# A decoder layer on one core: the first attention's steps dealt anew to the gaps between its groups' scores

## What is computed

```python
q = (x @ Wq).reshape(b, t, KV, G, D)
k = (x @ Wk).reshape(b, t, KV, D)
v = (x @ Wv).reshape(b, t, KV, D)
scores = jnp.einsum('bqhgd,bkhd->bhgqk', q, k) * scale
scores = jnp.where(causal_mask, scores, -jnp.inf)
w = jax.nn.softmax(scores, axis=-1)
y = jnp.einsum('bhgqk,bkhd->bqhgd', w, v)
x = _layernorm(x + y.reshape(b, t, H * D) @ Wo)
```

## Time and profile before

| | us |
|---|---|
| median of three runs | 1901.7 |
| the profiled execution | 1899.83 |
| its span | 1897.9 |
| TensorE busy | 1763.2 (93%) |
| VectorE busy | 1238.2 (65%) |
| ScalarE busy | 710.4 (37%) |
| GpSimd busy | 266.2 (14%) |

### The profile page before, as it was taken

How to read it: one execution, slowest core, us unless ns; L and a number is a source line. 1 busy time by engine, 2 the same in 40 slices (tenths; PEclk the granted TensorE clock), 3 DMA queues, 4 the chain that set the end, 5 groups by cost and what they waited for, 6 DMA issues and landing times.

```text
span 1897.9 us, 37020 instructions
## 1 busy us (share of the span) xinstructions
PE 1763.2 (93%) x14528; PEld 1448.6 (76%) x14528; DVE 1238.2 (65%) x1943; ACT 710.4 (37%) x1492; POOL 266.2 (14%) x237
## 2 busy tenths in 40 slices
PE   4888877799996999999999999999999999999997
PEld 3777765688885777878888888888888888888886
DVE  3667764668775556676676675665756766756776
ACT  4454542212121435353343343433433433434331
POOL 1444542534332000000000000000000000000000
PEclk8889988899998899999999999999999999999999
DMA  4111220100000203012020030020120200300011
GB/s 153 52 38 47 61 66 17 63 13 11 22 0 1 95 1 84 22 54 57 14 80 21 7 93 7 14 85 8 42 56 13 78 21 7 93 7 13 7 50 45
DMA packets 51082, 76.65 MB, mean 40 GB/s; under 512 B 9152, under 2 KB 27712, under 8 KB 50240
## 3 DMA queue, kind: packets, MB, share of 16 engines
q1 hardware_dynamic: 51008, 75.62, 13.3%
HBM read 68.78 MB, written 6.82 MB: 40 GB/s over the span
## 4 chain that ended last, share of the span: by engine, by line
PE 63%; DVE 2%; issue 2%; ACT 1%; POOLq 0%; POOL 0%; DVEq 0%
PE pair L1849 9%; PE pair L1850 9%; PE pair L1851 9%; PE y_ps L1849 3%; PE y_ps L1851 3%; PE y_ps L1850 3%; PE qa_ps L1849 3%; PE qa_ps L1851 3%; PE qa_ps L1850 3%; PE pair L1986 2%; PE pair L1977 2%; PE pair L1976 1%; PE pair L1985 1%; PE qd_ps L2053 1%; PE qd_ps L2054 1%
## 5 line engine op out<-in xcount | busy, mean ns | idle before, releaser
L1849 PE MATMUL pair<-XH,GUH 128*128 128x512 f32 x800 | 313.4, 392 | 0.0
L1850 PE MATMUL pair<-XL,GUH 128*128 128x512 f32 x800 | 312.3, 390 | 0.0
L1851 PE MATMUL pair<-XH,GUL 128*128 128x512 f32 x800 | 312.3, 390 | 0.0
L1849 PEld LDWEIGHTS pair<-XH,GUH 128*128 128x128 f32 x800 | 150.5, 188 | 32.3
L1851 PEld LDWEIGHTS pair<-XH,GUL 128*128 128x128 f32 x800 | 150.4, 188 | 32.2
L1850 PEld LDWEIGHTS pair<-XL,GUH 128*128 128x128 f32 x800 | 150.5, 188 | 31.6
L1413 POOL TENSOR_TENSOR qb_raw<-qb_raw,qb_scale 128x704 f32<-128x704 f32 x8 | 13.6, 1704 | 1057.7 <-DVE G L1567 923.4
L372 ACT ACTIVATE p<-scores_ps,nm 128x128 f32<-128x128 f32 (+1 forms) x256 | 104.1, 433 | 103.2 <-DVE nm L457 103.2
L1763 DVE TENSOR_TENSOR h<-pair,sg 128x512 f32<-128x512 f32 x80 | 55.2, 690 | 131.9 <-ACT sg L1512 130.2
L1423 ACT ACTIVATE HH<-h 128x512 fp32r<-128x512 f32 (+1 forms) x120 | 75.9, 633 | 170.5 <-DVE h L1768 94.0
L1567 DVE TENSOR_TENSOR HL<-h,HH 128x512 fp32r<-128x512 f32 (+1 forms) x120 | 83.4, 695 | 83.9 <-ACT HH L1423 83.9
(11 more groups left out here) (337 smaller groups left out, 4186.5 us busy)
## 6 DMA issues: line engine op xcount, KB each, us to landing
gu_raw<-in_gu SPq DMA_DIRECT2D x20, 512.0 KB, 3.8
wrep<-soft_f SPq DMA_DIRECT2D x64, 128.0 KB
dw_raw<-in_dw SPq DMA_DIRECT2D x10, 512.0 KB, 4.6
xT_raw<-in_xT SPq DMA_DIRECT2D x8, 512.0 KB, 4.1
x_raw<-in_x SPq DMA_DIRECT2D x8, 512.0 KB, 3.7
VR<-v_rows SPq DMA_DIRECT2D x32, 128.0 KB, 2.6
out<-xtok SPq DMA_DIRECT2D x4, 1024.0 KB, 4.3
gu_raw<-in_gu SPq DMA_DIRECT2D x10, 384.0 KB, 3.1
```

The lines of the kernel that those rows point to most:

```text
L1849: mm(out, wh, xh, start=first, stop=False)
L1850: mm(out, wh, xl, start=False, stop=False)
L1851: return mm(out, wl, xh, start=False, stop=last)
```

## The change

- **TensorE.** `vals(b)` and `queries(b, 1)` move into the batch itself, behind `scores(b, 0)`, followed by the transposes of batch b - 2. `values(b - 1)` moves behind `scores(b, 1)`. `queries(b + 1, 0)` and the first half of the output product stand behind `scores(b, 2)`, `keys(b + 1)` and the second half behind `scores(b, 3)`. `outputs` becomes `output(b, i)`, one half a call. Before the first scores stand `queries(0, 0)` and `keys(0)` alone.
- **VectorE.** The last group's work is finished in the next batch: `reciprocals(b - 1, 3, 1)` first of all, then `maxima(b, 0)`, the second residual of batch b - 2, and the probability turns of group 3. `probs_turned(b, 0, 0)` stands ahead of `reciprocals(b, 1, 1)`, `o_low` on both sides of `maxima(b, 2)`. The splits of the two weights for the next stage move from batch 0 to batch 1.
- **Semaphores.** `half_done` counts the first part of `values`, so that `probs_turned(b, 0, 0)` waits for that part and `probs_turned(b, 0, 1)` for the whole. `o_low` waits for its own `o_high`. `values` also waits for `values_copy`, the first queries of a batch for the first `o_low`, `context(1)` for the last `residual` of batch 6.
- **Banks.** Queries go to bank 0, keys and values to bank 1, output rows and their transposes to banks 2 and 3. `values` writes each bank's 256 columns in the order group, half, position, and `OH` and `OL` hold (group, half) blocks, so `o_high` and `o_low` each take two banks whole and no longer half of all four.
- **Queues.** ScalarE, GpSimd and SyncE follow the same order; `row_out` and `deviation` of the second half come a batch later. Batch 2 is unrolled too (the loop has 4 turns).

The core of the diff (a line "..." stands where lines are left out, removed ones among them):

```diff
@@ -150,7 +150,7 @@
 
         self.scores = ctx.enter_context(nc.psum_tensor("scores_ps", [P, 4, 512], F32))
         self.rest = ctx.enter_context(nc.psum_tensor("rest_ps", [P, 4, 512], F32))
-        self.projections = [self.rest[:, n, :] for n in (2, 3, 1)]
+        self.projections = [self.rest[:, n, :] for n in (1, 3, 2)]
         self.l_k, self.l_v, self.l_q, self.l_b = (ctx.enter_context(nc.semaphore("x_l_" + n)) for n in "kvqb")
         self.past = ctx.enter_context(nc.semaphore("past"))
...
 
         PB0, PB1 = sb("PB0", [P, G, KV * 4, 32]), sb("PB1", [P, G, KV * 8, 32])
-        OH, OL = sb("OH", [P, G, S], F32R), sb("OL", [P, G, S], F32R)
+
+        OH, OL = sb("OH", [P, G * 2, 4, 32], F32R), sb("OL", [P, G * 2, 4, 32], F32R)
         nm, sums, rinv = (sb(n, [P, 2, 8]) for n in ("nm", "sums", "rinv"))
         xs = sb("xs", [P, 2, D])
...
+
+        QB, KB = y_ps[:, 0, :], y_ps[:, 1, 0:S]
+
+        def have(b, n):
+            return not isinstance(b, int) or b >= n
+
+        def late(b, i):
+
+            return s_ps[:, i, :] if isinstance(b, int) and b == B - 1 else y_ps[:, 2 + i, :]
+
+        def turned(b, i):
+
+            if isinstance(b, int) and b >= B - 2:
+                bank = s_ps[:, 2 + i, :] if b == B - 1 else y_ps[:, 2 * i, :]
+            else:
+                bank = y_ps[:, 2 + i, :]
+            return bank.rearrange("p (c t) -> p c t", c=KC)
+
+        def values_ps(b):
+            return s_ps if isinstance(b, int) and b == B - 1 else y_ps
+
+        def two_blocks(t, h):
+
+            return t[:, :, 2 * h:2 * h + 2, :].rearrange("p x a j -> p a x j")
+
+        def two_banks(b, h):
+            return values_ps(b)[:, 2 * h:2 * h + 2, 0:S].rearrange("p a (x j) -> p a x j", j=32)
...
         def _(sp):
             def tokens(n, src):
-                sp.wait_ge(proj_done, NPJ * (n - 1) + 2)
+                sp.wait_ge(proj_done, NPJ * (n - 1) + 3)
                 alone(sp, past)
                 sp.dma_start(xT[:], src).then_inc(l_xt, 16)
 
...
@@ -271,26 +284,26 @@
                 sp.dma_start(x_in[:], A["x"][bass.ds(b * S, S), :].rearrange("(i p) n -> p i n", p=P)).then_inc(l_x, 16)
 
             def batch(b, nxt):
+                tokens(b + 1, nxt)
+                values_out(b)
+                if have(b, 2):
+                    residual_in(b - 1)
+                if isinstance(b, int) and b == 0:
+                    sp.dma_start(way.k_raw[:], A["xwk"]).then_inc(way.l_k, 16)
+                    sp.dma_start(way.v_raw[:], A["xwv"]).then_inc(way.l_v, 16)
+                    for g in range(4):
+                        sp.dma_start(way.qk_bias[32 * g:32 * g + 32, :, :], A["xbqk"]).then_inc(way.l_b, 16)
+                if isinstance(b, int) and b == B - 1:
+                    sp.wait_ge(proj_done, NPJ * B)
+                    sp.dma_start(way.q_raw[:], A["xwq"]).then_inc(way.l_q, 16)
                 values_in(b)
...
+
+            for b in range(2):
+                batch(b, A["xT"][:, :, (b + 1) * S:(b + 2) * S])
+            with sp.Fori(2, B - 1) as b:
+                batch(b, A["xT"][:, :, bass.ds((b + 1) * S, S)])
+            batch(B - 1, A["cT"][:, :, 0:S])
+            residual_in(B - 1)
 
         @block.gpsimd
...
@@ -314,27 +327,32 @@
                                         ALU.add).then_inc(xtok_rdy, 1)
 
             def batch(b, first, last):
+                if have(b, 1):
+                    divide(b - 1, 3, 1)
+                if have(b, 2):
+                    deviation(b - 2, 1)
                 divide(b, 0, 0)
+                if have(b, 2):
+                    row_out(b - 2, 1)
                 divide(b, 0, 1)
                 divide(b, 1, 0)
                 divide(b, 1, 1)
...
+                divide(b, 2, 0)
+                divide(b, 2, 1)
+                if have(b, 1):
                     deviation(b - 1, 0)
...
+                divide(b, 3, 0)
+                if have(b, 1):
+                    row_out(b - 1, 0)
+                if last:
+                    divide(b, 3, 1)
                     deviation(b - 1, 1)
...
                     row_out(b - 1, 1)
...
                     deviation(b, 0)
                     deviation(b, 1)
                     row_out(b, 0)
                     row_out(b, 1)
...
+            over_batches(pool, batch, 3)
 
...
@@ -390,47 +407,45 @@
 
             split_x(0)
             act.wait_ge(consts, 3)
...
+            copy(tri[:], tri_f[:]).then_inc(consts, 1)
+            copy(identR[:], ident[:]).then_inc(consts, 1)
             queries_high(0, 0)
...
             keys_high(0)
...
 
             def batch(b, first, last):
+                values_copy(b)
                 exps(b, 0, 0)
                 exps(b, 0, 1)
...
+                queries_high(b, 1)
+                if have(b, 2):
+                    features_out(b - 2, 0)
+                    features_out(b - 2, 1)
                 split_x(b + 1)
+                exps(b, 1, 0)
+                exps(b, 1, 1)
+                if have(b, 1):
+                    o_high(b - 1, 0)
+                    o_high(b - 1, 1)
                 if first:
                     weights_high(way.l_k, way.WKH, way.k_raw)
...
+                exps(b, 2, 0)
+                exps(b, 2, 1)
                 if first:
                     weights_high(way.l_v, way.WVH, way.v_raw)
...
                 if not last:
                     queries_high(b + 1, 0)
...
+                    keys_high(b + 1)
                 exps(b, 3, 0)
...
                 exps(b, 3, 1)
...
                 if last:
...
+                    features_out(b - 1, 0)
+                    features_out(b - 1, 1)
+                    o_high(b, 0)
+                    o_high(b, 1)
                     weights_high(way.l_q, WQH, way.q_raw)
...
+                    features_out(b, 0)
+                    features_out(b, 1)
+            over_batches(act, batch, 3)
 
         @block.vector
         def _(dve):
...
@@ -465,24 +480,22 @@
             def probs_turned(b, g, unit):
                 u = g % 2
                 dve.wait_ge(norm_rdy, 2 * (G * b + g) + unit + 1)
...
+                if g == 0:
+                    after(dve, (half_done, o_done)[unit], b)
                 probs, turned = ((p0, PB0), (p1, PB1))[unit]
                 nc.vector.transpose(turned[:, g], probs[:, u].rearrange("p v (c j) -> p (v c) j", j=32)).then_inc(pb_rdy, 1)
 
...
+            def o_low(b, h):
+                dve.wait_ge(oh_rdy, 2 * b + h + 1)
+                sub(two_blocks(OL, h), two_banks(b, h), two_blocks(OH, h).bitcast(F32)).then_inc(ol_rdy, 1)
+
+            def residual(b, i):
+                own = Steps(dve, dve_steps, 2, 2 * b + i)
                 dve.wait_ge(l_x, 16 * (b + 1))
                 after(dve, xtok_rdy, 2 * (b - 1) + i + 1)
...
@@ -503,65 +517,71 @@
             split_x(0)
             queries_low(0, 0)
             keys_low(0)
...
 
             def batch(b, first, last):
...
+                second = isinstance(b, int) and b == 1
+                if have(b, 1):
+                    reciprocals(b - 1, 3, 1)
                 maxima(b, 0)
...
+                if have(b, 2):
+                    residual(b - 2, 1)
+                if second:
+                    weights_low(0, way.WKH, way.WKL, way.k_raw)
+                if have(b, 1):
+                    probs_turned(b - 1, 3, 0)
+                if have(b, 2):
+                    norm_out(b - 2, 1)
+                if have(b, 1):
                     probs_turned(b - 1, 3, 1)
                 reciprocals(b, 0, 0)
+                queries_low(b, 1)
+                maxima(b, 1)
+                reciprocals(b, 0, 1)
+                split_x(b + 1)
+                reciprocals(b, 1, 0)
                 probs_turned(b, 0, 0)
...
+                if have(b, 1):
+                    probs_turned(b, 0, 1)
+                reciprocals(b, 1, 1)
+                if have(b, 1):
+                    o_low(b - 1, 0)
+                maxima(b, 2)
+                if have(b, 1):
+                    o_low(b - 1, 1)
+                else:
+                    probs_turned(b, 0, 1)
                 probs_turned(b, 1, 0)
...
+                reciprocals(b, 2, 0)
                 probs_turned(b, 1, 1)
...
                 reciprocals(b, 2, 1)
                 if not last:
                     queries_low(b + 1, 0)
                 maxima(b, 3)
...
+                if have(b, 1):
+                    residual(b - 1, 0)
+                probs_turned(b, 2, 0)
                 if not last:
                     keys_low(b + 1)
...
+                reciprocals(b, 3, 0)
+                if have(b, 1):
+                    norm_out(b - 1, 0)
+                probs_turned(b, 2, 1)
+                if second:
+                    weights_low(1, way.WVH, way.WVL, way.v_raw)
                 if last:
...
+                    reciprocals(b, 3, 1)
+                    probs_turned(b, 3, 0)
+                    residual(b - 1, 1)
+                    norm_out(b - 1, 1)
```

(54 more changed lines are left out.)

191 lines of the change are left out of this document (20 added, 171 removed).

## The result

| | before | after |
|---|---|---|
| median, us (four runs each) | 1901.32 | 1879.96 |
| lowest to highest | 1899.28 to 1902.15 | 1879.21 to 1881.12 |
| profiled execution, its span | 1899.83, 1897.9 | 1881.12, 1879.1 |

The account below looks back on a forecast made before the run. An order of hand-offs, with no engine full, bounds the kernel. 35.4 us to batch 7's first scores, 7.8 in batch 7 and 4 at the end make 47.2 off 1899.83: 1852.6, given as 1853; range 1843 to 1869.

Parts of the forecast that it names:

- Step 1 and 2: Loop batch: work dealt anew over TensorE's gaps, then waits between engines per cycle; 29.1 us a batch against 34.2.
- rival 2: TensorE's clock stays full: 0.6 us less in six batches and 1 more at the end, 1848; chance 0.15.
- its bad case: Loop batch, cycle 1: GpSimd's divide goes first, split_x stands 1.9 us, maxima of group 2 start some 1.2 late.
- Step 3, the start: Before the first scores: vals and second queries leave the way, 28.73 becomes 25.95, 2.8 us less; batch 0 takes 32.0.
- Step 3, batches 1, 2 and 3: Early attention batches: 29.1 us as in the loop, but 30.6 in batch 2, where a weight split delays maxima by 1.5.
- Step 4, batch 7 and the tail: End of the attention: 21.5 us against 29.3 to batch 7's fourth scores, 7.8 less, and 4 more from values(7) on.
- Rival 1: VectorE sets the pace in the loop batches: 31 us a batch for six batches, 11 less gained, 1864; chance 0.2.
- Rival 3: Loads of the next tokens set the pace, slower than before: needs landings of 13.1 us, at 14 1906; chance 0.03.
- Rival 4: Nothing comes of it: the freed gaps are spent elsewhere, a new wait of 5 us a batch; chance 0.02.

Follow-up runs that it names:

- the first experiment: The changed kernel with TensorE's loop from batch 2 on instead of 3, one batch fewer unrolled: 1872.9 us, ratio 0.9854 to the kernel before.
- Early steps moved: On top of the first experiment, a probability turn in batch 0, the second context weight's split and its copy moved: 1871.53 us, ratio 0.9834.
- The loop through batch 7: On top of Early steps moved, TensorE's loop turns from 2 to 7, with unread queries and keys of a ninth batch: 1856.45 us, ratio 0.9755.
- Filled as well: The loop through batch 7 with 44 unread products (88 instructions) in batch 0's idle stretches: 1864.22 us, ratio 0.9798.

## Why the prediction was wrong

Summed by the profiled executions the miss is 28.5 us (1881.12 against 1852.6).

- **Step 1 and 2, the work of the gaps and a batch of 29.1 us: right.** Measured 28.7: 7.45, 7.01, 7.22, 7.02 against 7.33, 7.04, 7.7, 7.04. The 5.34 us that the prediction kept for `values` were too many. Cycle 2 came out at 7.22 because `values` ran at full clock (rival 2's 28.5 a batch was nearer), so the turn waited for the `divide` and not for `values`. The `divide` beside `split_x` and the next one took 3.78 together; with 1.04 for the narrow one 2.74 are left for the wide one, the forecast's 2.8. `split_x` went first and took 1.19, as the forecast had it. The rule of the shared port pair (the Trainium skill, "SBUF — State Buffer", section "SBUF: two separate sides") agrees with that, and its bad case did not come.
- **Step 3, the start: right to 1.5 us.** The first `scores` came at 24.46 (forecast 25.95), and batch 0 took 31.71 (32.0).
- **Step 3, batches 1, 2 and 3: wrong by 6.4, 5.6 and 5.3 us** (35.50, 36.16 and 34.41 against 29.1, 30.6 and 29.1). The other repeated batches gave back 1.1.
- **Step 4, batch 7 and the tail: wrong by 7.5 and 5.7.** To its fourth `scores` batch 7 took 29.0 and not 21.5; from there to the second attention's first matmul it took 42.3, where the kernel before had 40.6 and the forecast, 4 less, 36.6. The last `values` stalled for 2.3 us, and half clock followed.
- **The term that failed** is the sentence "Loading instructions for one more unrolled batch I cost at nothing; no row prices it, and the range has 1 us for it". It was wrong in size (a batch with instructions that had not run cost 5.6 us more than a repeated one), and wrong in scope: not only the one more batch pays, but each of batches 1, 2, 3 and 7, and the tail. That new instructions are the cause is shown for batch 3 (5.6 us) and batch 7 (6.7); for batches 1 and 2 and the tail, which no run repeats, it rests on the same stalls, and of the 6.8 and 7.5 us that batches 1 and 2 stand above a repeated batch, 2.9 and 3.8 stayed when `values` no longer stalled. Some of that in batch 2 is the weight split at the end of batch 1: with it moved, the first cycle of batch 2 fell by 2.3, where the prediction had 1.5 for it. The forecast took the loop's batch 5 as the model of all, and so subtracted the idle 3.25 us before `values` from the first-time batches too, where it had a second use. Four batches at 5.3 to 7.5 and the tail make 30.5; with what went better (1.5 and 1.1 us, and 0.3 in batch 0) and 0.8 us lost later that is the miss, to 0.1.
- **It could have been seen.** In the trace of before, batch 1's `values` took 7.21 us after 3.27 of idle, against 5.42 in the earlier trace rows, and the first scores of batches 1, 2 and 3 stood 36.56 and 35.40 us apart against 34.2 later. I had read a loop batch alone, and the starts of batches 0 and 7. The row:

```profile
65.58 7.21 PE L643 MATMUL rest_ps<-PB,VR 32*32 32x128 f32 x288 [3.27 <-DVE PB L471]
```
- **The rivals.** Rival 1 is false in the repeated batches: VectorE waits for TensorE ahead of all four maxima of batch 4, by 0.33 to 0.83 us. Rival 3 is false: the loads land in 4.1 us, not 13. Rival 4 is false: 5.5 us came off each repeated batch. Rival 2 was right in the repeated batches and wrong everywhere else. No rival had the mechanism that decided, and the range had 1 us for it.

The Trainium skill ("Runtime: NRT & Kernel Launch", section "Instruction fetch mechanics") says that an engine's instructions are refilled in blocks of 16 KiB, 256 instructions. The packets and the pieces of 128 matmuls with their loads agree. It also says that the fetch is mostly hidden behind the rate of issue, and there the measurement decides: with 32x32 matmuls it is not hidden, it is 13.4 us of open stall in the changed kernel. And where it has kernels prefer full unrolling to branches, here a loop turn that repeats was the faster form, by 5.6 us for one batch.

**What stays open.** How the 5.6 us divide between the stall and the half clock behind it was not separated, since a stall is itself an idle of TensorE. How far ahead the pieces are fetched, and why the first cycles of batches 1 and 2 vary (7.2 to 10.05 us) with steps that should not touch them, was not settled. Nor was a second loss, in repeated turns: batch 5 of the first experiment, batches 3 and 5 of the runs "Early steps moved" and "The loop through batch 7" and batch 4 of "Filled as well" took 30.0 to 30.3 us and not 28.5 to 28.8. In each the third cycle took 8.7 us and not 7.2, at a granted clock of 0.80, with no stall and no instruction packet on TensorE's queue beside it. `values` with fewer instructions for the same amount of work was not measured.

## What to carry to other kernels

Read the first pass of every loop and each unrolled copy for itself. Where a stage is many small matmuls, its first run is bound by how fast instructions come (here 256 in 3.5 to 4 us), and an idle stretch ahead of it may be what hides that, so don't count the stretch as free. One more unrolled copy of such a stage cost 5.6 us here in its batch, and letting the loop take in the last batch, even with a little unread work, brought 7 us in that batch alone.

## What the runs showed of the hardware

- Instructions of TensorE that have not run before come in pieces of 256, with starts 3.5 to 4 us apart where TensorE uses them up faster. In repeated turns of a loop with some 1000 recorded matmuls and weight loads there were no instruction packets on its queue (batch 4 of the changed kernel, and the five repeated turns of "The loop through batch 7").
- The place of code within its piece was worth 5.7 us in a stage of small matmuls: 88 unrelated instructions, 44 products and their loads, some 500 us earlier made the same code 5.7 us slower, and a whole piece of 256 left it as it was.
- TensorE with half the products in `values` had the slower repeated batch, 30.7 against 28.7 us: behind the 3.17 us of idle that the missing work left its clock was at half.
- 32x32 matmuls at full clock started 14.8 ns apart (288 in 4.25 us), and 25 ns apart at half.
